# Stores of cells 0 to 4 on ScalarE's queue, the normalised input in three parts on SP's, clearings and statistics in another order

## The chip, the cores and the metric

The kernel runs on one core of a Trainium2 chip. The metric is the device time of one execution in microseconds (us), lower is better. In profiles PE is TensorE (PEld its weight loads), DVE is VectorE, ACT is ScalarE, POOL is GpSimd and SP is SyncE. SP, ACT and POOL can each issue DMAs; SPq, ACTq and POOLq are their issuing.

## The reference, cut to what matters

```python
x = x + _L0_conv_ref(_gn(x), L0_conv_W, L0_conv_b)      # the 4 x 4 lattice of cells, below
x = x + _L1_conv_ref(_gn(x), L1_conv_weight)            # 3 x 3 circular convolution
x = x + _L2_conv_ref(_gn(x), ...)                       # splines of the 3 x 3 patches
x = x + _L3_conv_ref(_gn(x), L3_conv_combinator, L3_conv_bias)
...
def _cell(w, bias, ins):                                # ins: 1 to 3 images of 16 channels
    x = jnp.concatenate(ins, axis=1)                    # (8, 48, 64, 64) after padding with zeros
    y = lax.conv_general_dilated(x, w, (1, 1), 'SAME')  # 3 x 3, 48 channels to 48
    y = jax.nn.relu(y + bias[None, :, None, None])
    right, up, down = jnp.split(y, 3, axis=1)
    return (right, up, down)
for col in range(4):
    for row in range(4):
        # column 0: the input, or the cell above's down; else right of the cell to the left,
        # up of the cell below (still of the column before) and down of the cell above
        outs[row] = _cell(W[col, row], b[col, row], ins)
```

x is (8, 16, 64, 64) in float32, `_gn` a group normalisation over two channels. The change is all in the first line, the lattice: 16 cells one behind another, each over 8 images.

## The kernel before

**Steps.** The lattice runs as 128 steps, step s = 8k + b for cell k = 4 * column + row and image b. A cell's kind is its number of inputs and of outputs that are used: cells 0 to 5 are "12", "13", "13", "12", "22", "33". Every image passes between cells through a scratch tensor `LAT` in HBM (`lattice` in the trace): a step loads its inputs from there with halos into a raw slot in SBUF, and stores its outputs to it. The loads of one step are 3, 6, 5, 3, 6 and 16 DMAs for cells 0 to 5 (`input_loads`), the stores 2, 1, 1, 2, 2 and 1 (`output_stores`).

**One step's way through the engines.** SP loads the raw slot (L795). ACT rounds it to fp32r, the high part (`split_hi`, L1136). DVE subtracts it from the raw values (the low part, L1437 or L1439 and L1440) and makes copies that stand in the other half of the partitions (L1449); `lo_ready` counts the low parts. PE multiplies (L1711) into four PSUM banks that go round. ACT evacuates each bank with bias and ReLU into a staging slot `ST` (`evacuate`, L1147). SP stores the slot (L778).

**Slots.** There are 4 raw slots of one half each (a "33" step takes two), 3 slots of split images, 4 banks and 3 staging slots. A load waits until DVE has read the slot's last user (four steps back, two for kind "33") and until image b of the cell before is stored. ACT, at step s, first waits until the store of step s - 3 has landed, then splits the piece two on, and then evacuates step s:

```python
if s >= SLOTS_S and (s - SLOTS_S) // B < NC - 1:
    z = s - SLOTS_S
    act.wait_ge(image_stored[z % B], 16 * stores_before[z // B + 1])
...
    split_hi(piece_step(ahead), ahead - pieces_before[piece_step(ahead)])   # ahead: two pieces on
    evacuate(s, range(h * part, (h + 1) * part))
```

**SP's queue** is written out in order. At step s it issues the loads of step s, then waits for the evacuation of step s - 4 (`STORE_LAG`) and issues its store. In some steps it loads raw weights too (L751).

**POOL** moves weights: at each step it waits for an evacuation, then issues its share of the next cell's weights (L892) or of the turned taps' stores (L884), and in cells 1 and 2 it clears 64 partitions of the four raw slots (L1011, counted by `kr_clear`). PE turns raw weights between steps, 18 small matmuls each (L1671).

**The start.** SP loads x in four parts. DVE clears the weight tile, the gaps of raw slots 0 and 1, and `XN`, the normalised input, which lies in raw slots 2 and 3. It forms the low part of cell 0's taps, then waits for the constants for `PAIR_MEAN`, and runs the eight `bn_stats` (L1361). PE, DVE and POOL turn them into mean and scale; ACT and DVE write the normalised input to `XN`. SP, which has first issued cell 0's weights (L760), stores images 0 and 1 of it to the lattice (L764, two DMAs of 272.5 KB), POOL the other six (L985, two of 817.5 KB). Step 0's and 1's loads wait for the first, the others for the second.

Of the kernel before, what the change touches and what calls it, by code (L numbers as in the profile page):

```python
# [6 lines left out]
P = 128  # L7
C = 16
# [3 lines left out]
B = 8  # L12
# [8 lines left out]
XPARTS = 4  # L21
FIRST = 2
BASES = 8
# [14 lines left out]
HOFF = EVEN  # L38
# [114 lines left out]
def build(nc, x, l0w, l0b, l1w, l2base, l2spline, l2scale, l2bias, l3w, l3bias, consts, out):  # L153
# [80 lines left out]
    with ctx:  # L234
# [3 lines left out]
        def sem(name):  # L238
            return ctx.enter_context(nc.semaphore(name))
# [124 lines left out]
        image_stored = [sem(f"image_stored{b}") for b in range(B)]  # L364
        input_stored = [sem(f"input_stored{i}") for i in range(2)]
        image_loaded = [sem(f"image_loaded{q}") for q in range(SLOTS_K)]
# [149 lines left out]
        def input_stores(i):  # L516

            rows = slice(0, FIRST * C) if i == 0 else slice(FIRST * C, P)
            for r in range(2):
                yield LAT[r * P + rows.start:r * P + rows.stop], XN[rows, r * PIECE:(r + 1) * PIECE]  # L520
# [223 lines left out]
        def _(sp):  # L744
# [17 lines left out]
            sp.wait_ge(xn_dve, 1)  # L762
            for dst, src in input_stores(0):
                sp.dma_start(dst, src).then_inc(input_stored[0], 16)  # L764

# [7 lines left out]
            def store_outputs(s):  # L773

                if s // B < NC - 1:
                    sp.wait_ge(evac_done, chunks_before[s + 1])
                    for dst, src in output_stores(s):
                        sp.dma_start(dst, src).then_inc(image_stored[s % B], 16)  # L778

            for s in range(STEPS):  # L780
                k, b = divmod(s, B)
                q, before = halves_before[s] % SLOTS_K, last_user[s]
                if before is not None and COPIES[cells[before // B].kind]:
                    sp.wait_ge(raw_read, copied_before[before + 1])
                elif before is not None:
                    sp.wait_ge(lo_ready, pieces_before[before + 1])

                if s == 4 * B:
                    sp.wait_ge(kr_clear, 4)
                if k == 0:  # L790
                    sp.wait_ge(input_stored[0 if b < FIRST else 1], 2 * 16)
                else:
                    sp.wait_ge(image_stored[b], 16 * stores_before[k])
                for dst, src in input_loads(s):
                    sp.dma_start(dst, src).then_inc(image_loaded[q], 16)  # L795
                if s >= STORE_LAG:
                    store_outputs(s - STORE_LAG)
                if (k, b) in RAW_STEPS:
                    sp.wait_ge(turned, TURN_AT[f"cell{RAW_STEPS[k, b] - 2}"])
                    load_taps(RAW_STEPS[k, b])  # L800
# [39 lines left out]
        def _(pool):  # L840

            pool.memset(TWOS[:, :], 2.0)
            pool.memset(NHALF[:, :], -0.5).then_inc(pool_const, 1)
            pool.memset(ST[:, :, :], 0.0).then_inc(st_clear, 1)
            pool.wait_ge(pool_const, 1)
# [135 lines left out]
            clear_taps("cell1")  # L981
            pool.wait_ge(xn_act, 1)
            pool.wait_ge(xn_dve, 1)
            for dst, src in input_stores(1):
                pool.dma_start(dst, src).then_inc(input_stored[1], 16)  # L985
            store_taps("cell1")
            for s in range(STEPS):
# [19 lines left out]
                if k == 5 and b == 7:  # L1007
                    kan_mask(range(4, 8))
                if k in (1, 2) and b in (1, 3):
                    half = 2 * (k - 1) + b // 2  # L1010
                    pool.memset(flat[4 * C:P, half * PIECE:(half + 1) * PIECE], 0.0).then_inc(kr_clear, 1)  # L1011
                if (k, b) in X_LOADS:
# [87 lines left out]
        def _(act):  # L1100
# [77 lines left out]
            for s in range(STEPS):  # L1178
# [8 lines left out]
                for h in range(cell.pieces):  # L1187
                    ahead = pieces_before[s] + h + 2
                    if ahead < TOTP:
                        split_hi(piece_step(ahead), ahead - pieces_before[piece_step(ahead)])  # L1190
                    evacuate(s, range(h * part, (h + 1) * part))
                if (k, b) in TURN_STEPS:
# [100 lines left out]
        def _(dve):  # L1293
# [3 lines left out]
            nc.vector.memset(WT[:, :, :].bitcast(F32), 0.0).then_inc(wt_clear, 1)  # L1297
            gaps = flat[:, 0:2 * PIECE].rearrange("p (t f) -> p t f", t=4)
            nc.vector.memset(gaps[:, :, LEAD:HOFF], 0.0)
            nc.vector.memset(XN, 0.0).then_inc(xn_clear, 1)  # L1300
# [13 lines left out]


            turned_lo_part("cell0")

# [29 lines left out]
            def tail(blk, b):  # L1347

                n = EVENT_AT[blk, b]
                if n > B:  # L1350
                    dve.wait_ge(norm_ready, n - B)
                group_stats(slice(n % B, n % B + 1), n)

            dve.wait_ge(const_loaded, 2 * 16)
            nc.vector.tensor_tensor(PAIR_MEAN.rearrange("p (b c) -> p b c", c=C),
                                    G[:, :].rearrange("p (b c) -> p b c", c=C),
                                    OWN.rearrange("p (b c) -> p b c", c=1).broadcast_to([P, B, C]), ALU.mult)
            for b in range(B):
                if b % 2 == 0:
                    dve.wait_ge(channel_loaded[b // 2], 16)  # L1360
                last = nc.vector.bn_stats(STATS[:, b], XC[:, b * PIX:(b + 1) * PIX])  # L1361
            last.then_inc(dve_step, 1)
# [535 lines left out]
```

## Time and profile before

| | |
|---|---|
| time, median of 3 runs | 1303.49 us (1298.91 to 1303.87) |
| the profiled execution, its own time | 1307.1 us |
| its span, first to last instruction | 1304.2 us |
| PE busy | 90% of the span |
| DVE, ACT, POOL busy | 59%, 51%, 29% |
| mean granted TensorE clock | 0.971 of full speed |
| DMA | 234.22 MB, mean 180 GB/s; SP's queue moved 207.02 MB |
| chain that ended last | PE 54%, SP's queue 16%, DVE 12%, DMA 6%, ACT 5% |

The profiler records one execution. The busy time of an engine is the time in which at least one of its instructions runs; "idle before" is the gap ahead of an instruction, with what ended it. The chain of waits is followed back from the last instruction, at each step to what released it. A granted clock of 1.00 is TensorE's upper level, 0.50 the lower.

### The profile page before, as it was taken

The page shows a single profiled execution, that of the slowest core. Times are in us where ns is not written, and L with a number is a line of the kernel's source. Part 1 is how long each engine was busy: PE and PEld are TensorE (multiplying, and loading weights), DVE is VectorE, ACT ScalarE, POOL GpSimd, SP SyncE. Part 2 cuts the span into 40 slices and gives each one's busy share as a digit, 9 for nine tenths or more (in the row PEclk, how much of TensorE's full clock was granted, in tenths as well). Part 3 has the DMA queues.
Part 4 walks back from the last instruction along what each step waited for, and adds up shares of the span by engine and source line. Part 5 has one row for each costly group of instructions (what it writes and reads, how often), then busy time and mean ns, then how long its engine had stood idle before and what let it go on. Part 6 is the DMA issues. An engine that isn't in the chain of part 4 may idle for free.

```text
span 1304.2 us, 14844 instructions
## 1 busy us (share of the span) xinstructions
PE 1179.5 (90%) x5088; PEld 874.7 (67%) x5088; DVE 772.4 (59%) x959; ACT 671.2 (51%) x720; POOL 382.3 (29%) x549
## 2 busy tenths in 40 slices
PE   1778999899999999989999999999999857999995
PEld 1645567666666677766666677877777645777773
DVE  5788972346656522236555552236665579899962
ACT  1567754335454444444454543434445498789821
POOL 5222532335420103321213213634134441103212
PEclk9989999899999999999999999999999878999998
DMA  6689988999999958889999987978799214677783
GB/s 177 167 212 237 270 245 236 197 178 178 217 208 207 221 167 211 223 189 211 196 204 185 194 226 202 252 203 227 192 209 178 47 25 71 94 116 112 117 125 57
DMA packets 106191, 234.22 MB, mean 180 GB/s; under 512 B 38388, under 2 KB 52292, under 8 KB 97668
## 3 DMA queue, kind: packets, MB, share of 16 engines
q1 hardware_dynamic: 89536, 207.02, 70.2%
q0 software_dynamic: 16032, 25.98, 10.5%
q8 instruction: 40, 0.66, 0.2%
q14 instruction: 35, 0.29, 0.1%
q10 hardware_dynamic: 548, 0.27, 0.1%
HBM read 124.15 MB, written 85.75 MB: 161 GB/s over the span
## 4 chain that ended last, share of the span: by engine, by line
PE 54%; SPq 16%; DVE 12%; DMA 6%; issue 5%; ACT 5%; POOL 1%; ACTq 0%; DVEq 0%; POOLq 0%
PE PB L1711 46%; SPq L795 13%; PE PB L1680 6%; DMA S<-lattice 2%; SPq L778 2%; ACT F L1136 2%; DMA lattice<-S 2%; DVE S L1548 2%; DVE S L1542 2%; DVE F L1535 1%; DVE S L1555 1%; DVE F L1437 1%; DMA F<-F 1%; DVE F L1449 1%; SPq L826 1%
## 5 line engine op out<-in xcount | busy, mean ns | idle before, releaser
L1711 PE MATMUL PB<-F,WA 128*96 128x512 f32 (+1 forms) x3792 | 923.8, 405 | 53.0 <-DVE F L1449 32.7
L1711 PEld LDWEIGHTS PB<-F,WA 128*96 128x96 f32 (+1 forms) x3792 | 665.7, 177 | 302.0 <-issue 49.4
L1136 ACT ACTIVATE F<-S 128x2116 fp32r<-128x2116 f32 (+4 forms) x160 | 261.7, 1636 | 240.9 <-issue 87.2
L1147 ACT ACTIVATE S<-PB,BIAS 96x512 f32<-96x512 f32 (+1 forms) x320 | 210.3, 680 | 280.3 <-PE PB L1711 279.9
L1437 DVE TENSOR_TENSOR F<-S,F 128x1089 fp32r<-128x1089 f32 (+2 forms) x80 | 121.4, 1518 | 189.7 <-ACT F L1136 189.3
L1439 DVE TENSOR_TENSOR F<-S,F 128x1058 fp32r<-128x1058 f32 x64 | 80.7, 1262 | 191.2 <-ACT F L1136 190.8
L1449 DVE CAST F<-F 64x528 fp32r<-64x528 f32 (+4 forms) x304 | 186.7, 663 | 3.5
L1680 PE MATMUL PB<-F,WA 128*128 128x512 f32 x576 | 149.5, 419 | 20.3 <-DVE F L1535 20.1
L892 POOL DMA_DIRECT2D WA<-taps x76 | 56.6, 746 | 340.0 <-ACT S L1147 321.7
L1680 PEld LDWEIGHTS PB<-F,WA 128*128 128x128 f32 x576 | 114.2, 200 | 49.9 <-issue 21.5
L1440 DVE TENSOR_TENSOR F<-S,F 64x1058 fp32r<-64x1058 f32 x64 | 82.0, 1281 | 0.0
L884 POOL DMA_DIRECT2D taps<-WX x112 | 67.9, 655 | 18.1 <-ACT S L1147 13.2
L859 POOL TENSOR_TENSOR RS<-VE,NHALF 128x1 f32<-128x1 f32 x25 | 24.4, 975 | 134.7 <-DVE VE L1335 134.6
L877 POOL MEMSET WX<- 48x1600 f32 x18 | 26.3, 1460 | 106.8 <-ACT S L1147 92.3
L1244 ACT ACTIVATE F<-S 128x2112 fp32r<-128x2112 f32 x16 | 31.5, 1967 | 27.8 <-DVE S L1555 14.9
L1443 DVE TENSOR_TENSOR F<-S,F 128x1089 fp32r<-128x1089 f32 x16 | 20.7, 1296 | 40.3 <-ACT F L1136 40.2
L1680 PE MATMUL PB<-F,WX 128*128 128x512 f32 x96 | 31.5, 490 | 13.6 <-DMA F<-F 13.6
L1119 ACT ACTIVATE KAN<-X,NBI,RS 64x512 f32<-64x512 f32 (+1 forms) x48 | 32.5, 676 | 20.2 <-POOL NBI L861 11.2
L1220 ACT ACTIVATE S<-KS,CB 128x528 f32<-128x528 f32 x64 | 41.8, 724 | 0.3
L1535 DVE SCALAR_TENSOR_TENSOR F<-S,F 128x1056 fp32r<-128x1056 f32 x32 | 38.9, 1259 | 3.6 <-ACT F L1244 3.6
L1080 POOL DMA_DIRECT2D out<-OT x26 | 14.7, 571 | 85.5 <-DVE OT L1523 85.5
L1542 DVE SCALAR_TENSOR_TENSOR S<-S 128x2112 f32<-128x2112 f32 x16 | 37.6, 2353 | 2.4 <-ACT S L1228 2.4
(125 smaller groups left out, 717.7 us busy)
## 6 DMA issues: line engine op xcount, KB each, us to landing
lattice<-S SPq DMA_DIRECT2D x48, 817.5 KB, 6.0
S<-lattice SPq DMA_DIRECT2D x448, 66.1 KB, 4.9
lattice<-S SPq DMA_DIRECT2D x98, 272.5 KB, 4.0
S<-lattice SPq DMA_DIRECT2D x160, 136.1 KB, 3.4
S<-lattice SPq DMA_DIRECT2D x72, 272.5 KB, 5.3
S<-lattice SPq DMA_DIRECT2D x160, 70.1 KB, 3.0
S<-lattice SPq DMA_DIRECT2D x80, 136.2 KB, 5.1
S<-lattice SPq DMA_DIRECT2D x160, 66.0 KB, 3.0
```

Source lines behind the costliest of these rows:

```text
L795: sp.dma_start(dst, src).then_inc(image_loaded[q], 16)
L884: pool.dma_start(dst, src).then_inc(tp_stored, 16)
L892: pool.dma_start(dst, src).then_inc(w_loaded[k % 2], 16)
L1136: act.activation(piece_view(s, h, 0), raw_view(s, h), ACT.Copy).then_inc(hi_ready, 1)
L1147: act.activation(wide(to[:, at:at + TS])[:, :, 0:RX], pixels(RING_BANK[n % SLOTS_O][0:cell.rows, :]), ACT.Relu, bias=BIAS[0:cell.rows, k:k ...
L1437: last = nc.vector.tensor_tensor(lo, raw, hi, ALU.subtract)
L1439: nc.vector.tensor_tensor(lo[:, 0:2], raw[:, 0:2], hi[:, 0:2], ALU.subtract)
L1440: last = nc.vector.tensor_tensor(lo[0:4 * C, 2:4], raw[0:4 * C, 2:4], hi[0:4 * C, 2:4], ALU.subtract)
L1449: last = nc.vector.tensor_copy(FP[4 * C:P, slot, part, to:to + n], FP[0:4 * C, slot, 0, source:source + n])
L1542: nc.vector.scalar_tensor_tensor(A2[n % 2], AA[n % 2], 2.0, A2[n % 2], ALU.subtract, ALU.mult)\
L1680: last = nc.tensor.matmul(pixels(bank[:, :]), weights, moving, start=open_ and n == 0, stop=close and n == len(todo) - 1)
L1711: last = nc.tensor.matmul(bank, WA[0:rows, first:first + cell.rows], wide(FZ[0:rows, i % SLOTS_F, base:base + TS])[:, :, 0:RX], start=j == ...
```

## The change

- **Stores.** The outputs of cells 0 to 4 are issued from ACT's queue instead of SP's: at step s, between the split and the evacuation, ACT stores step s - 1. From cell 5 on SP stores as before.
- **Normalised input.** SP issues all of it, in three parts: images 0 and 1, images 2 and 3, and, ahead of step 2's loads, images 4 to 7. Steps 0 and 1, 2 and 3, and 4 to 7 wait for their own part; step 2, whose loads overwrite `XN`, waits for the last one too.
- **Clearings.** POOL clears raw slots 0 and 1 whole at the very start (step 0's loads wait for it) and no longer clears slots in cells 1 and 2; DVE's clearing of the gaps is gone.
- **Statistics.** DVE's `bn_stats` come ahead of the low part of cell 0's taps (now behind the fourth) and of `PAIR_MEAN` (now behind the sixth).

```diff
--- before.py
+++ after.py
@@ -19,7 +19,8 @@
 YI = 8
 YB = 8
 XPARTS = 4
-FIRST = 2
+INPUT_PARTS = (0, 2, 4, 8)
+ACT_STORED = 5
 BASES = 8
 NJ = 2
 FEATS = BASES + 1
@@ -362,7 +363,7 @@
         l3_clear = sem("l3_clear")
 
         image_stored = [sem(f"image_stored{b}") for b in range(B)]
-        input_stored = [sem(f"input_stored{i}") for i in range(2)]
+        input_stored = [sem(f"input_stored{i}") for i in range(3)]
         image_loaded = [sem(f"image_loaded{q}") for q in range(SLOTS_K)]
         tp_stored = sem("tp_stored")
         w_loaded = [sem("w_loaded0"), sem("w_loaded1")]
@@ -515,7 +516,7 @@
 
         def input_stores(i):
 
-            rows = slice(0, FIRST * C) if i == 0 else slice(FIRST * C, P)
+            rows = slice(INPUT_PARTS[i] * C, INPUT_PARTS[i + 1] * C)
             for r in range(2):
                 yield LAT[r * P + rows.start:r * P + rows.stop], XN[rows, r * PIECE:(r + 1) * PIECE]
 
@@ -760,8 +761,9 @@
                 sp.dma_start(dst, src).then_inc(w0_loaded, 16)
             sp.wait_ge(xn_act, 1)
             sp.wait_ge(xn_dve, 1)
-            for dst, src in input_stores(0):
-                sp.dma_start(dst, src).then_inc(input_stored[0], 16)
+            for i in range(2):
+                for dst, src in input_stores(i):
+                    sp.dma_start(dst, src).then_inc(input_stored[i], 16)
 
             def l1_halos(j):
 
@@ -772,7 +774,7 @@
 
             def store_outputs(s):
 
-                if s // B < NC - 1:
+                if ACT_STORED <= s // B < NC - 1:
                     sp.wait_ge(evac_done, chunks_before[s + 1])
                     for dst, src in output_stores(s):
                         sp.dma_start(dst, src).then_inc(image_stored[s % B], 16)
@@ -780,15 +782,19 @@
             for s in range(STEPS):
                 k, b = divmod(s, B)
                 q, before = halves_before[s] % SLOTS_K, last_user[s]
+                if s == 0:
+                    sp.wait_ge(kr_clear, 1)
                 if before is not None and COPIES[cells[before // B].kind]:
                     sp.wait_ge(raw_read, copied_before[before + 1])
                 elif before is not None:
                     sp.wait_ge(lo_ready, pieces_before[before + 1])
-
-                if s == 4 * B:
-                    sp.wait_ge(kr_clear, 4)
+                if k == 0 and b == 2:
+                    for dst, src in input_stores(2):
+                        sp.dma_start(dst, src).then_inc(input_stored[2], 16)
                 if k == 0:
-                    sp.wait_ge(input_stored[0 if b < FIRST else 1], 2 * 16)
+                    sp.wait_ge(input_stored[b // 2 if b < 4 else 2], 2 * 16)
+                if s == 2:
+                    sp.wait_ge(input_stored[2], 2 * 16)
                 else:
                     sp.wait_ge(image_stored[b], 16 * stores_before[k])
                 for dst, src in input_loads(s):
@@ -841,6 +847,7 @@
 
             pool.memset(TWOS[:, :], 2.0)
             pool.memset(NHALF[:, :], -0.5).then_inc(pool_const, 1)
+            pool.memset(flat[:, 0:2 * PIECE], 0.0).then_inc(kr_clear, 1)
             pool.memset(ST[:, :, :], 0.0).then_inc(st_clear, 1)
             pool.wait_ge(pool_const, 1)
 
@@ -979,10 +986,6 @@
             store_taps("cell0")
             norm(slice(1, 2), slice(0, 1), 1)
             clear_taps("cell1")
-            pool.wait_ge(xn_act, 1)
-            pool.wait_ge(xn_dve, 1)
-            for dst, src in input_stores(1):
-                pool.dma_start(dst, src).then_inc(input_stored[1], 16)
             store_taps("cell1")
             for s in range(STEPS):
                 k, b = divmod(s, B)
@@ -1006,9 +1009,6 @@
                     kan_mask(range(4))
                 if k == 5 and b == 7:
                     kan_mask(range(4, 8))
-                if k in (1, 2) and b in (1, 3):
-                    half = 2 * (k - 1) + b // 2
-                    pool.memset(flat[4 * C:P, half * PIECE:(half + 1) * PIECE], 0.0).then_inc(kr_clear, 1)
                 if (k, b) in X_LOADS:
                     load_x(X_LOADS[k, b])
                 if k + 1 < NC and k != 12:
@@ -1188,6 +1188,10 @@
                     ahead = pieces_before[s] + h + 2
                     if ahead < TOTP:
                         split_hi(piece_step(ahead), ahead - pieces_before[piece_step(ahead)])
+                    if h == 0 and 0 < s <= ACT_STORED * B:
+                        act.wait_ge(evac_done, chunks_before[s])
+                        for dst, src in output_stores(s - 1):
+                            act.dma_start(dst, src).then_inc(image_stored[(s - 1) % B], 16)
                     evacuate(s, range(h * part, (h + 1) * part))
                 if (k, b) in TURN_STEPS:
                     turned_hi_part(TURN_STEPS[k, b])
@@ -1295,8 +1299,6 @@
 
 
             nc.vector.memset(WT[:, :, :].bitcast(F32), 0.0).then_inc(wt_clear, 1)
-            gaps = flat[:, 0:2 * PIECE].rearrange("p (t f) -> p t f", t=4)
-            nc.vector.memset(gaps[:, :, LEAD:HOFF], 0.0)
             nc.vector.memset(XN, 0.0).then_inc(xn_clear, 1)
 
             def clear_weights():
@@ -1312,8 +1314,6 @@
                 nc.vector.tensor_tensor(taps_view(name, 1), turned_view(name), taps_view(name, 0).bitcast(F32),
                                         ALU.subtract).then_inc(turned_lo, 1)
 
-
-            turned_lo_part("cell0")
 
             def squares(cols):
 
@@ -1351,13 +1351,20 @@
                     dve.wait_ge(norm_ready, n - B)
                 group_stats(slice(n % B, n % B + 1), n)
 
-            dve.wait_ge(const_loaded, 2 * 16)
-            nc.vector.tensor_tensor(PAIR_MEAN.rearrange("p (b c) -> p b c", c=C),
-                                    G[:, :].rearrange("p (b c) -> p b c", c=C),
-                                    OWN.rearrange("p (b c) -> p b c", c=1).broadcast_to([P, B, C]), ALU.mult)
+            def pair_means():
+
+                dve.wait_ge(const_loaded, 2 * 16)
+                nc.vector.tensor_tensor(PAIR_MEAN.rearrange("p (b c) -> p b c", c=C),
+                                        G[:, :].rearrange("p (b c) -> p b c", c=C),
+                                        OWN.rearrange("p (b c) -> p b c", c=1).broadcast_to([P, B, C]), ALU.mult)
+
             for b in range(B):
                 if b % 2 == 0:
                     dve.wait_ge(channel_loaded[b // 2], 16)
+                if b == 4:
+                    turned_lo_part("cell0")
+                if b == 6:
+                    pair_means()
                 last = nc.vector.bn_stats(STATS[:, b], XC[:, b * PIX:(b + 1) * PIX])
             last.then_inc(dve_step, 1)
             dve.wait_ge(dve_step, next(steps))
```

## Rows read from the trace of the kernel before

**Rows 1.** Stretches: us, busy time (x instructions) of each engine, granted PE clock, DMA share, GB/s

```profile
38.10:79.76 41.66, 33.85 (x134) 24.83 (x135) 30.94 (x31) 22.40 (x27) 8.74 (x13) 0.92 0.68 176
79.76:167.78 88.02, 75.93 (x336) 49.64 (x337) 82.26 (x64) 64.57 (x79) 32.89 (x34) 1.00 0.96 249
167.78:198.75 30.97, 25.79 (x115) 19.40 (x114) 20.22 (x21) 17.05 (x23) 10.97 (x13) 1.00 0.87 238
198.75:254.16 55.41, 49.50 (x211) 39.04 (x211) 13.72 (x14) 22.97 (x28) 11.59 (x17) 0.94 0.88 219
254.16:314.30 60.14, 57.82 (x243) 39.61 (x244) 36.60 (x44) 24.67 (x25) 25.07 (x38) 0.94 1.00 175
```

**Rows 2.** The chain of waits in order of time: start us, us, what

```profile
21.41 4.36 DMA lattice<-S
...
28.14 5.97 DMA S<-lattice
...
112.33 1.97 SPq L795
...
409.91 83.84 PE PB L1711 x352
```

**Rows 3.** The timeline, PE: start us, us, instruction, [idle before <- what ended it]

```profile
72.75 11.93 PE L1711 MATMUL PB<-F,WA 128*96 128x512 f32 x40 [6.68 <-DVE F L1449]
...
254.15 42.00 PE L1711 MATMUL PB<-F,WA 128*96 128x512 f32 x168 [5.91 <-DVE F L1449]
```

**Rows 4.** The timeline, SP's queue, in cell 1

```profile
64.31 4.25 SPq L795 DMA_DIRECT2D S<-lattice  x6
...
111.24 0.58 SPq L778 DMA_DIRECT2D lattice<-S  x1
```

**Rows 5.** The timeline, SP's queue, at the change to cell 5

```profile
231.51 12.64 SPq L795 DMA_DIRECT2D S<-lattice  x16
...
256.17 2.26 SPq L778 DMA_DIRECT2D lattice<-S  x2
...
280.18 1.23 SPq L778 DMA_DIRECT2D lattice<-S  x2
```

**Rows 6.** The timeline, ACT, in cell 5

```profile
293.74 1.98 ACT L1136 ACTIVATE F<-S 128x2116 fp32r<-128x2116 f32 x1 [10.30 <-DMA lattice<-S]
```

**Rows 7.** The timeline, all engines, at the start

```profile
0.73 1.85 SPq L747 DMA_DIRECT2D X<-in_x  x4
...
0.80 5.55 POOL L844 MEMSET S<- 128x6543 f32 x1
...
1.19 0.44 ACTq L1102 DMA_DIRECT2D IDF<-in_consts  x1
...
15.47 5.19 SPq L760 DMA_DIRECT2D WA<-taps  x8
```

**Rows 8.** The timeline, ACT, a step of cell 1 and one of cell 3

```profile
95.41 2.02 ACT L1136 ACTIVATE F<-S 64x2180 fp32r<-64x2180 f32 x1 [1.61 <-issue]
97.33 2.39 ACT L1147 ACTIVATE S<-PB,BIAS 96x512 f32<-96x512 f32 x4
...
178.28 1.11 ACT L1136 ACTIVATE F<-S 64x1089 fp32r<-64x1089 f32 x1 [3.87 <-DMA S<-lattice]
179.30 1.24 ACT L1147 ACTIVATE S<-PB,BIAS 128x512 f32<-128x512 f32 x2
```

**Rows 9.** The timeline, DVE, then POOL, in cells 1 and 2

```profile
98.32 2.41 DVE L1437 TENSOR_TENSOR F<-S,F 64x2180 fp32r<-64x2180 f32 x1
100.76 2.56 DVE L1449 CAST F<-F 64x2180 fp32r<-64x2180 f32 x3
...
130.80 4.15 DVE L1449 CAST F<-F 64x2180 fp32r<-64x2180 f32 x3
...
130.57 1.91 POOL L1011 MEMSET S<- 64x2180 f32 x1 [3.40 <-ACT S L1147]
```

**Rows 10.** DMA issues from 80 to 180 us: count, size, median us from issue to landing

```profile
lattice<-S SPq DMA_DIRECT2D x16, 817.5 KB, 6.0
```

## The prediction, made before the changed kernel ran

> **What bounds the kernel now.** The page says that TensorE (PE) is busy for 90% of the span, but the share is an average over stages, so I cut the first 314 us at steps. A step is one image of one cell (step 8k + b); its matmuls are 12, 20, 20, 12, 24 and 56 for cells 0 to 5, by `terms`. Counting them on PE's timeline puts step 0 at 38.10 us, step 9 at 79.76, step 24 (cell 3) at 167.78, step 32 (cell 4) at 198.75, step 40 (cell 5) at 254.16 and step 44 at 314.30. [rows 1] are the five stretches; their counts are the steps' 116, 300, 96, 192 and 224 matmuls plus 18 for each turning of weights. Where nothing holds PE, 352 matmuls take 83.84 us [rows 2], 0.238 each. So pure work would be 27.6, 71.4, 22.8, 45.7 and 53.3 us, and the excess over it is 14.0, 16.6, 8.1, 9.7 and 6.8 us, 55 in all. Six turnings, about 1.3 us each, are in it and stay. About 47 us can be won at most behind the first matmul. After 314 us PE hardly stops until the last column, and the change touches nothing there.
>
> What holds PE in each stretch: before step 8 it idles 6.68 us [rows 3], because cell 1's loads come late. SP's queue is full without a gap there: six loads 4.25 us, then a store [rows 4]. Behind an 817 KB store the second load's issue takes 1.97 us [rows 2], against 4.25 / 6 = 0.71 for an ordinary one; that store thus costs SP 0.58 + 1.3, not 0.58. In steps 9 to 23 three engines are near their limit beside SP: DVE is busy 82.26 of 88.02 us, the DMA engines 0.96 [rows 1]. Before cell 5, PE idles 5.91 us [rows 3]: ScalarE stands in order at `split_hi` for step 40's sixteen loads, which took 12.64 us of issue [rows 5]. Then ScalarE waits for stores of cell 4: step 37's is issued at 256.17 and step 39's at 280.18 [rows 5], behind loads four steps on, although PE had done step 39 by 248.2 [rows 3]. ScalarE sits idle for both, 10.30 us for the second [rows 6].
>
> **The change, part by part.**
>
> Start. The statistics begin before the constants, so normalising ends sooner, but SP's own eight weight DMAs last from 15.47 to 20.66 [rows 7] and the input stores start at 21.05 (their transfer is in [rows 2] from 21.41). The reordering of DVE and POOL is thus worth at most 0.4 us; I take 0.2. POOL's new first clearing (4360 columns, by the 6543 in 5.55 us [rows 7] 3.7 us) is hidden: it all ends near 10.1, when the first taps are turned. What changes is traffic: 0.54 MB for images 0 and 1, then as much for 2 and 3, instead of 0.54 plus POOL's 1.64 MB at once. Before, the stores took 4.36 us to land and step 0's last load 5.97 [rows 2], though the loads of an idle queue land in about 3. I take the stores landing 1 us sooner, three issues 1 us shorter and the load landing 3 us sooner: first matmul at 33.1 instead of 38.1. Against it, SP issues the last part only behind step 1's loads (about 28.3), and step 2 waits until it has landed (about 6 us for 1.09 MB, 34.4), then for its loads (38.2) and the 4 us from split to matmul: 42.2, against 46.1 before (the 25th matmul of the timeline). Net 4 us; bounds 6 (no second wait) and -3 (the congestion stays and the wait comes on top).
>
> Steps 3 to 8. SP no longer issues two stores a step (1.1 to 1.2 us), and ScalarE does. Its step becomes 1.11 split + 1.24 evacuation [rows 8] + 1.1 store = 3.5, with gaps 3.6 us, over PE's 2.9. Step 7 then starts at 42.2 + 5 x 3.6 = 60.2; step 8's split, subtraction and copies are twice as wide and add 2.3: 66.1; step 9 at 71.0 instead of 79.76. **Stretch 1: 8.8 us** with the start in it; bounds 2 and 11.
>
> Steps 9 to 23. SP falls from 5.9 to some 4 us a step. Next come DVE, 2.41 + 2.56 [rows 9] = 5.0; PE 4.8; ScalarE 2.02 + 2.39 less 0.1 overlap [rows 8] + 0.6 = 4.9. So 15 steps cannot take under 76 us. The four clearings by POOL go too: one lay at 130.57, and the copies beside it took 4.15 instead of 2.56 us [rows 9]; 4 x 1.5 = 6 us of DVE time goes, in steps where DVE had no idle time. With three engines at 5.0 in order of each other and the DMA engines near full, I take 5.35 a step and 2.5 for turnings: 82.8. **Stretch 2: 5.2 us**; bounds 0 (engines full) and 10.
>
> Cell 3. ScalarE at 3.6 a step, 28.5 in all against 30.97. **2.5 us**; bounds -3 and 5.
>
> Cell 4. PE needs 45.7 + 1.9, and SP, at 3.7 a step without stores, now waits for slots instead of running late. Step 40's loads can start about 5 us sooner relative to PE (at 231.51 they stood behind a store and step 39's loads), so most of the 5.91 idle and of the half-speed time behind it goes (granted clock 0.94 in the stretch [rows 1]). 49 against 55.41. **6.4 us**; bounds 2 and 8.
>
> Cell 5 to step 43. Stores of cell 4 leave from ScalarE one step after evacuation, some 20 us sooner than 280.18, so both waits go. Step 43's start was held by them for 2.3 us, and the clock fell. But the DMA engines are at 1.00 here [rows 1] with POOL's spline weights. **4 us**; bounds 0 and 5.7.
>
> Later: ACT_STORED ends at cell 5, so SP's order is as before; PE works through. The extra wait at step 32 falls away and cost nothing. 0.
>
> Price of a store on ScalarE: one DMA issue on its queue at the start took 0.44 us while SP issued four in 1.85 [rows 7]; SP's large store took 0.58 [rows 4], and the worst comparable issue 1.97 [rows 2]. I take 0.6, since ScalarE's queue would hold one store at a time, which lands in 6.0 us [rows 10], a little over a step.
>
> Sum: 8.8 + 5.2 + 2.5 + 6.4 + 4 = 26.9. All three floors of stretch 2 lie within 0.2 us of each other, so I round down to 25. The profiled execution took 1307.1 (span 1304.2 and 2.9 around it) and comes to 1282; the median, 1303.49, lies 3.6 lower, so 1278.5, say 1279.
>
> **The rivals.**
>
> A, chance 0.14: the transfers bind, not the issuing. For it: DMA shares of 0.96 and 1.00 in stretches 2 and 5 [rows 1]. Against it: 0.68, 0.87 and 0.88 in the others, and an SP queue that is full while PE idles. Stretch 2 could shrink by 4% (3.5), stretch 5 not at all, the rest give 4 + 3 + 1 + 1: 12.5 us, 1291. The Trainium skill (DMA: Bandwidth & Descriptors, Issuing engines are not separate DMA queues) states that issuing from several engines only saves issue time, usually small beside the transfer. By that rule the time would be near this rival's; in stretches 1 and 4 the trace speaks against it.
>
> B, chance 0.07: the start turns bad, because step 2's new wait is long and loads 0 and 1 don't hurry: -3 instead of +4, the rest as forecast: 1286.
>
> C, ending on the other side, chance 0.08: a store's issue on ScalarE takes as long as SP's stalled one. ScalarE does split and evacuation in order, so everything behind it waits: the next evacuation, by it PE's bank, and two steps on the next split. For an issue of x us, steps 9 to 23 cost 4.3 + x: at 1.97 it is 6.3 against 5.87, a loss of 6; cells 0 and 3 (two DMAs) lose as much; cells 4 and 5 still give 8 and the start 4: about 1302, no change. From x = 2.5 on it is slower by over 0.5%; at 2.8, 1312. Against it: 0.44 beside a busy SP [rows 7]. The Trainium skill (Perfetto Trace Analysis, DMA Instruction — HWDGE) says that the descriptor generator is locked for exclusive use, and a DMA instruction's profiled time includes the wait for the lock. By that rule ScalarE would inherit part of SP's 1.97 us stalls; no row of before shows both queues under load.
>
> D, chance 0.03: nothing moves, since what PE lacks is DVE's copies alone: 1302.
>
> **How the numbers follow.** The forecast has 0.68: 1279, own range 1267 to 1289. The range that leaves out no more than 2 in 10 reaches from 1267 (all upper bounds but the start's) to 1295, past A and B. I call 0.5% (6.5 us) what a measurement here can tell. Forecast, A and B are faster, but A's lower part and half of C and D fall within it: faster 0.86, same 0.08, slower 0.06.
>
> **What would show it.** PE's first matmul near 33 and a gap before step 2; step 9 near 71, step 24 near 154, step 32 near 182, step 40 near 231, step 44 near 287; SP with idle time in cells 3 and 4; ScalarE's store issues at 0.4 to 0.7 us; no copies of 4 us beside an L1011 clearing; no wait of 10 us of ScalarE for stores of cell 4. The prediction is wrong if those issues take over 1.5 us, if stretch 2 keeps 88 us, or if ScalarE waits for its own stores three steps back.

## The result, and the profile after

| | before | after |
|---|---|---|
| median, us | 1303.68 (1298.91 to 1304.85, 4 runs) | 1286.55 (1284.67 to 1288.86, 4 runs) |
| ratio after / before | | 0.9891, 95% [0.9866, 0.9917] |
| profiled execution: time, span, us | 1307.1, 1304.2 | 1285.85, 1284.0 |

The kernel is 17.1 us faster by the medians. The forecast was 1279, so the gain came out at 17 us instead of 25. Where the two traces part can be read with the same cuts as in [rows 1]: counting matmuls on TensorE's timeline puts steps 0, 9, 24, 32, 40 and 44 at 36.93, 76.05, 158.87, 185.06, 237.45 and 292.86 us. These are the stretches of the changed kernel; the columns are those of [rows 1].

```profile
36.93:76.05 39.12, 33.10 (x135) 24.33 (x135) 29.92 (x31) 25.06 (x30) 9.44 (x13) 0.96 0.87 228
76.05:158.87 82.82, 74.64 (x337) 49.95 (x337) 76.69 (x64) 63.15 (x77) 25.04 (x30) 1.00 0.97 264
158.87:185.06 26.19, 25.07 (x116) 19.67 (x114) 19.64 (x21) 17.16 (x23) 10.57 (x13) 1.00 0.95 271
185.06:237.45 52.39, 48.27 (x211) 37.74 (x211) 13.72 (x14) 23.78 (x29) 11.59 (x17) 1.00 0.92 241
237.45:292.86 55.41, 54.84 (x243) 37.41 (x244) 36.23 (x43) 24.53 (x25) 25.75 (x38) 1.00 1.01 175
```

Step 44 starts 314.30 - 292.86 = 21.4 us sooner, and the span is 20.2 us shorter: nothing more was won behind it, as forecast. Of the 21.4 us, the start and cells 0 and early 1 gave 3.7 (79.76 - 76.05), steps 9 to 23 gave 5.2, cell 3 gave 4.8, cell 4 gave 3.0 and cell 5 up to step 43 gave 4.7. A second trace of the changed kernel (the run called the changed kernel again, below) cuts into 5.4, 5.1, 3.2, 5.3 and 3.4, so apart from steps 9 to 23 a single stretch is known to some 2 us only. The column to look at is the last one: in steps 9 to 23 the DMA engines were as good as full before (0.96) and are now (0.97), yet they move 264 GB/s instead of 249, the same 21.9 MB in both. A busy share near 1 did not mean that no more would go through.

TensorE's timeline at the start and at the change to cell 5:

```profile
36.93 8.10 PE L1718 MATMUL PB<-F,WA 128*128 128x512 f32 x24 [15.46 <-DVE F L1456]
46.95 3.10 PE L1718 MATMUL PB<-F,WA 128*128 128x512 f32 x12 [1.93 <-DVE F L1456]
...
68.10 6.50 PE L1718 MATMUL PB<-F,WA 128*96 128x512 f32 x20 [2.64 <-DVE F L1456]
...
237.44 13.48 PE L1718 MATMUL PB<-F,WA 128*96 128x512 f32 x56 [2.64 <-DVE F L1456]
```

The first matmul is 1.2 us sooner, not 5. Step 2 waits 1.93 us and then starts 0.8 us later than before. The wait ahead of cell 1 has shrunk from 6.68 to 2.64 us and the one ahead of cell 5 from 5.91 to 2.64 [rows 3].

The start is in the chain of waits:

```profile
14.40 1.86 DMA taps<-WX
...
21.63 0.52 SPq L766
22.19 5.59 DMA lattice<-S
...
28.17 2.02 SPq L801
...
32.65 6.54 DMA lattice<-S
...
40.07 2.75 DMA S<-lattice
```

Before, the chain passed in the same place through ScalarE's normalising, and the input stores began at 21.05, when that ended:

```profile
18.69 2.34 ACT S L1119 x3
```

Now normalising ends at 19.0 (it starts at 15.90 and lasts 3.1), but SP's weight loads, which start at 16.28 instead of 15.47, end at 21.51, and the input stores wait for them. What the new order of the statistics wins is lost again in SP's queue. The stores then take 5.59 us to land instead of 4.36 [rows 2]. The third part takes another 6.54, and only then do step 2's loads go.

SP's queue in cells 1 and 2 and in cell 4, and ScalarE in cell 1:

```profile
89.58 34.99 SPq L801 DMA_DIRECT2D S<-lattice  x32
...
199.34 62.73 SPq L801 DMA_DIRECT2D S<-lattice  x80
```

```profile
91.32 2.02 ACT L1136 ACTIVATE F<-S 64x2180 fp32r<-64x2180 f32 x1 [3.79 <-issue]
91.34 0.31 ACTq L1194 DMA_DIRECT2D lattice<-S  x1
93.24 2.39 ACT L1147 ACTIVATE S<-PB,BIAS 96x512 f32<-96x512 f32 x4
95.52 2.02 ACT L1136 ACTIVATE F<-S 64x2180 fp32r<-64x2180 f32 x1
...
180.24 3.94 ACTq L1194 DMA_DIRECT2D lattice<-S  x2
184.22 1.27 ACT L1147 ACTIVATE S<-PB,BIAS 128x512 f32<-128x512 f32 x2 [2.99 <-PE PB L1718]
```

Two things are to be seen. An 817 KB store takes ScalarE's queue 0.31 us, and it starts 0.02 us after a split that runs for 2.02: the issue lies beside the activation, so a step of ScalarE still takes 95.52 - 91.32 = 4.2 us, as without a store. And SP's queue has no gap in these two rows, although the stores have left it: 1.09 us a load in the first row, 0.78 in the second. (Such a row of a queue would also join issues with a wait between them; here each issue starts 0.04 to 0.10 us behind the last. At the start there are waits, up to 1.8 us near 50.) Before, the same queue looked like this:

```profile
93.69 5.14 SPq L795 DMA_DIRECT2D S<-lattice  x6
98.87 0.58 SPq L778 DMA_DIRECT2D lattice<-S  x1
...
216.21 3.73 SPq L795 DMA_DIRECT2D S<-lattice  x6
219.99 1.09 SPq L778 DMA_DIRECT2D lattice<-S  x2
```

In cell 4 a step took SP six loads at 0.62 and a store, 5.0 us with the gaps between; now six loads at 0.79 (39 loads in the first 30.87 us of its row), 4.7 us. In cells 1 and 2 it was 0.945 a load (27 loads in 25.51 us of issue between 93.69 and 122.59) beside 0.7 for a store. Those two windows are not the same steps; over all of steps 9 to 23, the issues alone, a load took 0.94 us before and 1.02 after (1.07 in the second trace). There 11.1 us of store issues left SP's queue, and the issues of loads grew from 71.4 to 75.6 us. So SP got back only part of what the stores had cost it. The rest went into longer issues of the loads.

ScalarE's own idle time tells what its splits waited for. In cells 0 to 3, in both kernels, every wait of more than 0.2 us ahead of a split ended 0.07 us (once 0.38) behind the landing of a load, and the last store had landed 0.29 us or more before. So neither kernel waited there for staging slots, nor did moving the stores help by freeing them sooner.

### The profile page after: what moved, and what is told of

Same layout as the page of the kernel before. It is cut to its first block, busy times and chain, and to the rows that moved or that the text cites. A ratio compares the mean times of both kernels' runs of the same rounds, so it can differ in the third digit from the quotient of the medians.

```text
span 1284.0 us, 14847 instructions
## 1 busy us (share of the span) xinstructions
PE 1169.6 (91%) x5088; PEld 867.4 (68%) x5088; DVE 766.1 (60%) x958; ACT 672.5 (52%) x720; POOL 378.6 (29%) x544
## 4 chain that ended last, share of the span: by engine, by line
PE 61%; SPq 14%; DVE 12%; issue 5%; DMA 4%; ACT 3%; POOL 1%; DVEq 0%; ACTq 0%; POOLq 0%
PE PB L1718 53%; SPq L801 11%; PE PB L1687 6%; DMA S<-lattice 2%; DVE S L1555 2%; DVE S L1549 2%; DVE F L1542 1%; DVE S L1562 1%; DMA F<-F 1%; PE PB L1678 1%; SPq L832 1%; DMA lattice<-S 1%; DVE F L1444 1%; ACT F L1136 1%; DVE F L1456 1%
## 5 line engine op out<-in xcount | busy, mean ns | idle before, releaser
L1456 DVE CAST F<-F 64x528 fp32r<-64x528 f32 (+4 forms) x304 | 179.7, 640 | 3.5
## 6 DMA issues: line engine op xcount, KB each, us to landing
S<-lattice SPq DMA_DIRECT2D x72, 272.5 KB, 4.9
lattice<-S SPq DMA_DIRECT2D x52, 272.5 KB, 4.3
lattice<-S ACTq DMA_DIRECT2D x48, 272.5 KB, 5.0
```

Of the source, the lines that this page charges most:

```text
L1456: last = nc.vector.tensor_copy(FP[4 * C:P, slot, part, to:to + n], FP[0:4 * C, slot, 0, source:source + n])
```

## The experiments

The theory was that SP's issuing held cells 0 to 4, so that the stores are the gain. Its rivals: that the transfers bind (A); that VectorE's copies beside the clearings were the brake; that the start gives or takes several us. The runs were made in three sets, and each ratio is to the kernel before of its own set, whose medians were 1301.0, 1301.38 and 1301.4 us.

**The changed kernel again.**

> The changed kernel once more, as the mark for the runs beside it: 1284 to 1289 us by every theory.

1283.92 us (1278.27 to 1289.38), 0.9871 [0.9844, 0.9897]: the gain repeats, in a later set. Its trace starts step 0 at 36.62, step 9 at 74.32, step 24 at 157.28, step 32 at 185.06, step 40 at 235.18 and step 44 at 291.89. Its first stretch:

```profile
36.62:74.32 37.70, 32.04 (x134) 23.83 (x135) 29.89 (x31) 24.14 (x29) 9.41 (x13) 1.00 0.87 237
```

**The stores alone**, in the kernel before.

```diff
-                if s // B < NC - 1:
+                if ACT_STORED <= s // B < NC - 1:            # ACT_STORED = 5
...
+                    if h == 0 and 0 < s <= ACT_STORED * B:
+                        act.wait_ge(evac_done, chunks_before[s])
+                        for dst, src in output_stores(s - 1):
+                            act.dma_start(dst, src).then_inc(image_stored[(s - 1) % B], 16)
```

> The kernel before with one part of the change alone: outputs of cells 0 to 4 issued from ScalarE's queue. Start, clearings and order of the statistics as before. Theory (the whole gain is SP's relief by the stores; the new start is worth nothing): 1284 to 1289 us, as the changed kernel's 1286.6, perhaps 2 more for the four clearings. Rival (the new start carries 4 to 5 us of it, as forecast): 1291 to 1293.

1283.45 us (1277.74 to 1289.05), 0.9883 [0.9843, 0.9923]. The stretches of steps 9 to 23 and of cell 3:

```profile
73.61:155.48 81.87, 75.05 (x337) 49.84 (x338) 79.47 (x64) 63.40 (x77) 32.80 (x34) 1.00 0.97 268
155.48:180.54 25.06, 25.06 (x116) 19.67 (x114) 19.86 (x21) 17.23 (x23) 10.76 (x13) 1.00 0.95 279
```

The whole gain is the stores'. In cell 3 TensorE is busy for 25.06 of 25.06 us. With the old start, step 0 begins at 38.90, step 2 at 46.23 without a gap, and step 9 at 73.61: 2.4 us sooner than in the first trace of the changed kernel and 0.7 sooner than in the second. VectorE, with the clearings in, is busy for 79.47 of 81.87 us in steps 9 to 23, and the stretch is not longer for it.

**The start alone**: the changed kernel with SP's stores as before.

```diff
-ACT_STORED = 5
+ACT_STORED = 0
```

> The changed kernel with all stores back on SP's queue, so the input in three parts, the clearings and the order of the statistics alone. Theory: 1301 to 1305 us, no change against before's 1303.7. Rival (the start is worth its share): 1297 to 1299.

1302.47 us (1298.47 to 1303.84), 1.0005 [0.9988, 1.0023]. TensorE's timeline:

```profile
36.89 7.95 PE L1718 MATMUL PB<-F,WA 128*128 128x512 f32 x24 [15.41 <-DVE F L1456]
46.41 3.11 PE L1718 MATMUL PB<-F,WA 128*128 128x512 f32 x12 [1.57 <-ACT F L1136]
...
73.03 12.29 PE L1718 MATMUL PB<-F,WA 128*96 128x512 f32 x40 [7.32 <-DVE F L1456]
```

The first matmul is as early as in the changed kernel, step 2 waits for the third part, and the wait ahead of cell 1 is 7.32 us. The new start is worth nothing by itself, together with the clearings and the order of the statistics that go with it.

**GpSimd clears again in cells 1 and 2**: the changed kernel with the four clearings put back, on top of its new one.

```diff
+                if s == 4 * B:
+                    sp.wait_ge(kr_clear, 5)
...
+                if k in (1, 2) and b in (1, 3):
+                    half = 2 * (k - 1) + b // 2
+                    pool.memset(flat[4 * C:P, half * PIECE:(half + 1) * PIECE], 0.0).then_inc(kr_clear, 1)
```

> The changed kernel with GpSimd's four clearings of raw slots in cells 1 and 2 put back; step 32's loads wait for them. Theory (in steps 9 to 23 the transfers bind, and VectorE has 6 us to spare in 82.8): 1286 to 1289 us. Rival (VectorE's copies bind there, each clearing costs 1.5 us): 1291 to 1293.

1283.79 us (1279.39 to 1288.37), 0.9872 [0.9834, 0.991]. VectorE, then GpSimd:

```profile
76.93 4.39 DVE L1461 CAST F<-F 64x2180 fp32r<-64x2180 f32 x3
81.35 2.42 DVE L1449 TENSOR_TENSOR F<-S,F 64x2180 fp32r<-64x2180 f32 x1
83.80 2.56 DVE L1461 CAST F<-F 64x2180 fp32r<-64x2180 f32 x3
```

```profile
76.99 1.91 POOL L1016 MEMSET S<- 64x2180 f32 x1 [15.86 <-ACT S L1152]
```

Three copies beside a clearing take 4.39 us, and 2.56 without one: the stretching that the prediction read in [rows 9] is real, 1.83 us for a clearing of 1.91. It costs nothing here, so VectorE is not what holds this stretch. The Trainium skill (SBUF — State Buffer, Who interferes with whom) states that a VectorE instruction in a mode that takes the pair of ports shared with GpSimd, which a cast can enter, and a GpSimd instruction block each other for the whole instruction; the rows agree with that in size.

**A quarter more bytes from ScalarE**: the changed kernel with a second store behind each of the sixteen of cells 1 and 2, 24 rows of 2180 elements (209,280 bytes) to a tensor that nobody reads. Its reuse of the staging slot is guarded by a wait of its own.

```diff
+                        if B <= s - 1 < 3 * B:
+                            at = (s - 1 - B) * 24
+                            act.dma_start(SPARE[at:at + 24], staged(s - 1)[0:24, 1:1 + 2 * SEG]).then_inc(spare[(s - 1) % SLOTS_S], 16)
```

> The changed kernel; each output of cells 1 and 2 has a quarter of its rows (204 KB) stored once more to a spare tensor, from ScalarE's queue, 16 DMAs and 3.3 MB in all. Theory (the DMA engines bind steps 9 to 23, at 264 GB/s): 12 us more, 1297 to 1301. Rival (ScalarE, VectorE and TensorE, all near 5 us a step, bind and the transfers have room): 0 to 3 us more, 1287 to 1290.

1304.02 us (1299.25 to 1310.0), 1.003 [1.0004, 1.0056]. That costs 20 us over its neighbours in this set (1283.45 and 1283.79), more than any theory had. It left open whether it was the bytes, the second issue with its wait, or the narrow shape. Two further runs part these.

**The same issues with 1 KB each**, and **the same bytes in 96 rows of 545 elements** (again 209,280 bytes each, 3.35 MB in all).

```diff
-                            act.dma_start(SPARE[at:at + 24], staged(s - 1)[0:24, 1:1 + 2 * SEG])...
+                            act.dma_start(SPARE[at:at + 16], staged(s - 1)[0:16, 1:1 + 16])...      # first
+                            act.dma_start(SPARE[at:at + 96], staged(s - 1)[0:96, 1:1 + 545])...     # second
```

> The control to the run with a quarter more traffic: the same 16 extra DMAs from ScalarE's queue and the same waits, but each of only 16 rows by 16 columns (1 KB). Theory (the bytes cost, not the issues and waits): within 2 us of the changed kernel. Rival (ScalarE pays for each more DMA and wait): 8 to 18 us more, as with 204 KB.

> The changed kernel with 16 extra stores of 96 rows by 545 columns (209 KB, a quarter more again), a shape that divides among all 16 DMA engines as the output's own does; 24 rows do not. Theory (transfers bind, 264 GB/s): 11 to 14 us more than the changed kernel, less than the 17 of the 24-row form, whose bytes lay on fewer engines. Rival (the 17 us were the uneven share alone): 0 to 4 us more.

1279.88 us (1277.31 to 1292.56), 0.9855 [0.982, 0.9889], and 1293.36 us (1290.35 to 1295.35), 0.9939 [0.9917, 0.9961]. Steps 9 to 23 of the first, then of the second:

```profile
74.66:157.92 83.26, 77.02 (x338) 52.09 (x337) 76.08 (x64) 64.18 (x78) 25.19 (x30) 0.96 0.99 264
```

```profile
73.55:165.70 92.15, 77.88 (x337) 52.01 (x337) 74.92 (x62) 64.00 (x78) 25.41 (x30) 0.94 0.97 268
```

Sixteen more issues and waits cost nothing: 1279.88 lies 4 us under the changed kernel's 1283.92, and the intervals overlap. The bytes cost 9.4 us beside the changed kernel and 13.5 beside the small ones. In the stretch, 268 x 92.15 against 264 x 83.26 is 2.7 MB more in 8.9 us more, and 2.7 MB at 268 GB/s would be 10. The cost arrives through SP's queue, for its loads take 1.15 us each in this stretch, the issues alone, instead of 0.95. So with the stores on ScalarE's queue it is the transfers that hold steps 9 to 23. No run takes loads off SP's queue there, so whether its issuing adds something of its own is not shown. The Trainium skill (DMA: Bandwidth & Descriptors, Issuing engines are not separate DMA queues) states that several issuing engines share the same DMA engines and save issue time alone; for this stretch, now, the runs agree. Of the 20 us of the 24-row form, about half is thus its shape: by the same page of the Trainium skill (Why a DMA increments its semaphore by 16 and not by 1) a transfer is spread over the largest number up to 16 that divides its outer size, which gives 12 for 24 rows and 16 for 96. The two runs agree with that, but do not show the engines.

**Each store right behind its own evacuation**, not one step later behind the next split.

```diff
-                    if h == 0 and 0 < s <= ACT_STORED * B:
-                        act.wait_ge(evac_done, chunks_before[s])
-                        for dst, src in output_stores(s - 1):
-                            act.dma_start(dst, src).then_inc(image_stored[(s - 1) % B], 16)
...
+                if s < ACT_STORED * B:
+                    act.wait_ge(evac_done, chunks_before[s + 1])
+                    for dst, src in output_stores(s):
+                        act.dma_start(dst, src).then_inc(image_stored[b], 16)
```

> The changed kernel; ScalarE issues the store of step s right behind the evacuation of step s, not behind the next step's split. Theory (transfers bind steps 9 to 23): the stores leave 2 to 4 us sooner and the time stays within 3 us of the changed kernel. Rival (the wait for the staging slot's store three steps back binds): 4 to 8 us less.

1286.43 us (1279.83 to 1291.35), 0.9887 [0.9861, 0.9914]: no gain from stores that start sooner. Staging slots do not hold the kernel either, as ScalarE's waits said above.

**Cells 0 to 3 alone from ScalarE**, and **cell 4 alone**; the rest from SP.

```diff
-ACT_STORED = 5
+ACT_STORED = 4
```

```diff
-                if ACT_STORED <= s // B < NC - 1:
+                if s // B < NC - 1 and s // B != 4:
...
-                    if h == 0 and 0 < s <= ACT_STORED * B:
+                    if h == 0 and 4 * B < s <= ACT_STORED * B:
```

> The changed kernel with ScalarE storing cells 0 to 3 alone; cell 4's stores are SP's again, behind loads four steps on. Theory (cell 4's stores from ScalarE end the waits at the turn to cell 5, worth the 3.0 + 4.7 us won in the last two stretches of the profile after): 1289 to 1293 us. Rival (that gain comes from SP being ahead after cell 3): 1284 to 1287.

> The changed kernel with ScalarE storing cell 4 alone; cells 0 to 3 are SP's. Theory: 6 to 9 us of the 17 are left, 1293 to 1296 us. Rival (the order of the stores of cell 4 matters only when SP is ahead): 1299 to 1303.

1285.5 us (1280.84 to 1290.5), 0.9879 [0.985, 0.9908], and 1299.91 us (1297.79 to 1303.44), 0.999 [0.9974, 1.0006]. ScalarE at the beginning of cell 5 when SP stores cell 4, and TensorE there when only cell 4 is ScalarE's:

```profile
248.01 1.98 ACT L1136 ACTIVATE F<-S 128x2116 fp32r<-128x2116 f32 x1 [9.53 <-DMA lattice<-S]
...
261.05 1.98 ACT L1136 ACTIVATE F<-S 128x2116 fp32r<-128x2116 f32 x1 [6.90 <-DMA lattice<-S]
```

```profile
255.20 41.74 PE L1718 MATMUL PB<-F,WA 128*96 128x512 f32 x168 [8.08 <-DVE F L1456]
```

The first falsifies the idea that cell 5 gains because ScalarE no longer waits for SP's late stores: ScalarE waits for them as long as ever (9.53 and 6.90 us, against 10.30 in [rows 6]), and the time is the changed kernel's. TensorE does idle for 2.04 us ahead of step 41 there, but only 1.19 ahead of step 40, where the changed kernel has 0.56 and 2.64. The second removes exactly these waits and gains 1.5 us by the medians, within its interval, with 8.08 us of idle time ahead of cell 5. What pays there is that SP has issued step 40's loads well before TensorE ends step 39, and it does so because of cells 0 to 3: the lead is 4.1 us before, 3.7 with cell 4 alone and 3.8 with the start alone, but 8.2 with cells 0 to 3, 8.2 with the stores alone and 7.7 in the changed kernel.

**The third part stored by GpSimd**, beside SP's first two, so that step 2 need not wait behind SP's loads.

```diff
-                if k == 0 and b == 2:
-                    for dst, src in input_stores(2):
-                        sp.dma_start(dst, src).then_inc(input_stored[2], 16)
...
+            pool.wait_ge(xn_act, 1)
+            pool.wait_ge(xn_dve, 1)
+            for dst, src in input_stores(2):
+                pool.dma_start(dst, src).then_inc(input_stored[2], 16)
```

> The changed kernel with the normalised images 4 to 7 stored by GpSimd beside SP's first two parts, not by SP behind step 1's loads. Theory (step 2's wait for the last part takes back what the earlier first load gives; 2.1 us idle ahead of step 2): the gap before step 2 goes, the first matmul is a little later, 0 to 3 us less than the changed kernel. Rival (all of the input's 2.2 MB must pass first in any order): no change.

1285.63 us (1282.98 to 1289.39), 0.9881 [0.9857, 0.9906]:

```profile
39.70 10.39 PE L1719 MATMUL PB<-F,WA 128*128 128x512 f32 x36 [18.22 <-DVE F L1457]
```

Steps 0, 1 and 2 now run in one piece, but from 39.70 on, so step 2 is where it was: it starts at 46.13, 46.95 and 47.05 us in the kernel before, the changed kernel and this one. In all three the 2.2 MB of the input pass before step 2, and how they are cut only moves the wait.

**All cells from ScalarE**: the kernel of the stores alone with its bound raised.

```diff
-ACT_STORED = 5
+ACT_STORED = 15
```

> The stores-only kernel (old start) with all cells' stores from ScalarE's queue, 0 to 14. Theory (SP's relief matters also where its queue is full: cells 12 and 13, with six to nine loads and four stores a step): 3 to 6 us less than with cells 0 to 4, 1277 to 1281 us. Rival (TensorE binds from cell 5 on, as forecast): no change, 1283 to 1286.

1285.27 us (1277.78 to 1288.41), 0.9863 [0.9829, 0.9896]: from cell 5 on there is nothing to win by it, and the theory of 3 to 6 us is wrong. No version tried beats the changed kernel by more than the intervals.

## Why the prediction was right, and which terms were mis-sized

The direction, the place and the mechanism were right: SP's queue held cells 0 to 4, and taking the stores off it is the whole gain (the stores alone give 0.9883, the start alone 1.0005). The sum was 26.9 by terms, cut to 25. The trace gave 21.4, the medians 17. What was mis-sized is the start together with steps 3 to 8, at 8.8 us for a measured 3.7 (5.4 in the second trace), and the issue time of the loads, which was taken as fixed. It is in part luck that the sum came as near as it did: in the first trace cells 3 and 5 gave more than I had, the start and cell 4 less.

| term | forecast | trace | second trace | what the runs showed |
|---|---|---|---|---|
| start to step 9 | 8.8 | 3.7 | 5.4 | the start gives nothing, the stores alone 6.2 |
| steps 9 to 23 | 5.2 | 5.2 | 5.1 | held by transfers, not by VectorE |
| cell 3 | 2.5 | 4.8 | 3.2 | a store costs ScalarE next to nothing |
| cell 4 | 6.4 | 3.0 | 5.3 | loads' issues grew |
| cell 5 to step 43 | 4 | 4.7 | 3.4 | not through ScalarE's waits |

**Start.** This is the largest miss. "I take the stores landing 1 us sooner" turned out the other way: 5.59 us instead of 4.36 [rows 2]. SP now sends four of them in a row, and GpSimd's second group of tap stores runs beside them from 21.35 on (23.27 before); no run parts the two. They also start 0.6 us later (21.63 against 21.05), where I had 0.2 sooner, since the first tap stores start at 10.72 instead of 9.93 and SP's weight loads follow them. The loads of step 0 did hurry: they begin 2 us later, and ScalarE's first split, which waits for them, starts 1.2 us sooner (32.96 against 34.13). The wait ahead of step 2 was foreseen, but I had step 2 at 42.2 and it starts at 46.95, since the third part began 4 us later than I had it (32.09, behind the later loads). So of the bounds of 6 and -3, rival B's -3 was nearer than my +4: at step 2 the trace has -0.8, and at step 9 the stores with the old start are 79.76 - 73.61 = 6.2 us ahead of before, those with the new one 3.7. Between these two single traces lie 2.4 us against the new start, but the second trace of the changed kernel halves that and more (0.7), and between the medians there is nothing. Steps 3 to 8, at 4.8 in the forecast, gave 4.5 in the first trace and 6.3 with the stores alone, so that term was about right.

**Steps 9 to 23** came out to the tenth, but partly for the wrong reason. I had VectorE, TensorE and ScalarE in turn at 5.0 us a step. VectorE's 6 us beside the clearings went, and they are worth nothing, for with them put back the time stays. What sets 5.52 us a step are the transfers. So rival A's mechanism holds here, with a price that I had at 3.5 us of gain and that was 5.2, because 249 GB/s at a share of 0.96 was not yet the end.

**ScalarE's price of a store.** I took 0.6 us in series with split and evacuation. The issue runs beside the split, so it is near 0, and cell 3 could fall under the 28.5 us that I had for it (8 steps of 3.6 would be 28.8): 26.19. Rival C (issues of 2 us and more that block ScalarE) is seen three times, 2.00 us at 60.79, 2.79 at 176.10 and 3.94 at 180.24, and behind the last two the evacuations idled for 1.87 and 2.99 us. That is over the 1.5 us that I gave as a sign of being wrong, in three of forty steps. The two in cell 3 are no chance: the second trace has them again, 2.17 at 176.89 and 3.78 at 180.40. In the first, single loads that SP issues beside them take 2.2 and 2.9 us. They don't decide the time, for cell 3 is shorter all the same. The Trainium skill (Perfetto Trace Analysis, DMA Instruction — HWDGE) has a descriptor generator that is locked for exclusive use; such a lock may be behind these, which no run here shows. In cells 1 and 2 SP's stalls did not reach ScalarE: SP's loads took up to 2.96 us there and none of ScalarE's stores over 0.37.

**Cell 4.** I expected SP to stand idle at 3.7 us a step. It has no gap: six loads now take 4.7 instead of 3.7. The idle time of TensorE ahead of cell 5 went from 5.91 to 2.64 and not to nearly nothing. How much of the 3.4 us between forecast and trace this explains stays open, for the second trace, with loads as long, has 5.3. The issues of the loads also grew in cells 1 and 2, and this is why the gain is smaller than the stores' issue time taken off SP.

**Cell 5.** The size is right and the cause was not: ScalarE's waits for SP's late stores [rows 5, 6] go, but they cost the kernel nothing that can be measured, as the runs with cells 0 to 3 alone and cell 4 alone show. The gain is the full clock (1.00 instead of 0.94 in [rows 1]) and TensorE at work for 54.84 of 55.41 us, since SP comes to cell 5 ahead.

What stays open is why the medians give 17 and the two profiled executions 21: the profile of before was 3.4 us above its median, and the changed kernel's own runs spread by 4 us here and by 11 in a later set.

## What to carry to other kernels

If one queue issues loads and stores and has no gap while TensorE waits, move the stores to an engine that runs long instructions: the issue hides beside them, as 0.31 us did here beside a split of 2.02. Don't credit the queue with the whole issue time of what leaves it, for the remaining issues may grow until the transfers are what binds. A wait that is long on a side engine is worth what TensorE loses by it, and that is read at TensorE, not there.

## What the runs showed of the hardware that was not expected

- The issue of a load on SP has no fixed price: 0.62 us in cell 4 before, 0.79 after, and 0.945 and 1.09 in cells 1 and 2, with the same shapes. It grows with the traffic of another queue: 0.95 us in steps 9 to 23 with 1 KB stores more on ScalarE's queue, 1.15 with as many of 209,280 bytes (96 rows).
- A DMA share of 0.96 at 249 GB/s and one of 0.97 at 264 GB/s are the same traffic at two speeds; cell 3 reached 279 GB/s at 0.95 with the stores alone. The share did not tell how near the limit was.
- A DMA issue on ScalarE's queue takes 0.31 to 0.37 us for 817 KB, where SP's took 0.58, and lies beside ScalarE's running activation. Two stores of 272.5 KB mostly took 1.1 us there, where SP's took 1.1 to 1.3, and twice in cell 3, in both traces, 2.2 to 3.9.
- Sixteen stores of 209,280 bytes cost some 20 us as 24 rows and 9 to 14 us as 96 rows.
